# Attention and mixture-of-experts block on one core: routing arithmetic in the rank bank, plain fp32 products, and a re-laid order of slots and transfers

## The chip, the core and the metric

One core of one Trainium2 chip runs the whole program. The metric is the device time of one execution in microseconds (us), the median of several runs. The hardware profiler recorded one more execution of the kernel before.

## What is computed

128 sequences of 128 rows with 256 features: a layer norm, differential cross-attention onto a context (16 heads, 32 half-heads of 8 dimensions), a residual, a second layer norm, and a mixture of 16 experts with two chosen per row, plus a shared expert.

```
x = x + xattn(ctx, layernorm(x))   # att = softmax(q1 k1) - lam * softmax(q2 k2), 16 heads
scores = sigmoid(h @ gate_w.T)                           # h = layernorm(x), 16 experts
topk_w, topk_idx = top_k(scores, 2)
topk_w = topk_w / (topk_w.sum(-1) + 1e-20) * 2.5
routed = sum over the two experts of w * (silu(h @ w_gate) * (h @ w_up)) @ w_down
shared = silu(h @ ws_gate) * (h @ ws_up) @ ws_down
x = x + routed + shared
```

## The kernel before

The program has two stages. The first takes the 128 sequences two at a time: 64 **steps**, software-pipelined over every engine. The second runs 144 tiles of expert rows, twice.

In a step each engine walks 16 **slots** k = 0 to 15 (`step`, one function for each engine). On TensorE a slot is four score matmuls of sequence pair `it` and four matmuls of pair `b` = it+1 whose maxima VectorE takes (`both`, L477 and L470), then `attend` every second slot (L510), then `side`: the work of other pairs that is hung on this slot. ScalarE takes the exponential of a slot's scores (L783) and then its own side work; VectorE the maxima (L916) and side work. Each engine runs its list strictly in order. The letters: `a` = it+3 (projection of queries and keys), `xs` = it+4 (first norm), `n2`, `k2` = it+2, `d` = it-1 (second norm, transposes), `r` = it-2 (routing, shared expert, scatter).

Four PSUM banks carry side work: M0 and M1 (`ms_ps`), OT and TO (`o_ps`). `clear` makes TensorE wait until the previous user of a bank has been read. TO holds in turn the transposed outputs, the transposed maxima and the **rank bank** contents: the matmuls of L617 and L618 give every row its rank among the rows of its expert, and the totals.

Routing of pair r: ScalarE's exp (`ez`), VectorE's `best_two` (slot 2), `choice` (slot 3, one-hot rows `hot`, and `hots`, signed by the direction in which an expert's list grows), TensorE's ranks (slot 5), `places` (slot 6) and `positions` (slot 8), then four indirect DMAs by GpSimd (`scatter`). Several small VectorE operations read and write SBUF alone: `den`, `hots`, `hotp`.

Products of the first stage are made of three single-pass fp32r matmuls of high and low parts (`product`, L538 to L540), the shared expert's gate and up and the router's logits among them; VectorE makes the low part `h_lo` for these.

Queries and keys are cut into three bf16 parts: ScalarE writes the first, GpSimd the second (L1230) and third (L1232), SyncE puts them to DRAM (`put_parts`) and loads them as stacks (`load_stacks`). The row maxima go into the stacks as two more rows (`put_max`, from `mxT`, which ScalarE copies at slots 2 and 11). Slot 8 of TensorE waits for the DMA semaphores of both:

```
if k % 4 == 0:
    wait(pe, d_stk[u][1 - k // 4 % 2], STK, b, STK)
wait(pe, v_red, NCH, b, k - 1)
...
if do_c and k % (NCH // 2) == 0:
    wait(pe, d_m[u], MR, it, MR)
```

## Time and profile before

| | us |
|---|---|
| median of 3 runs (2449.36 to 2455.13) | 2450.85 |
| the profiled execution, its own time | 2456.25 |
| its span | 2454.5 |
| TensorE busy, share of the span | 2113.0, 86% |
| VectorE busy | 1754.8, 71% |
| GpSimd busy | 1494.5, 61% |
| ScalarE busy | 1406.2, 57% |

TensorE's matmuls overlap each other, so that its busy time is the time in which at least one was under way. The granted clock is the share of full TensorE speed (2.4 GHz) that the chip gave: 1.0 or, for stretches, 0.5. The idle time in a row is what the engine stood still right before these instructions, and the names behind the arrow say what ended it. A step ends where the next one's first exponential starts.

### The profile page before, as it was taken

How to read it: one execution, taken by the hardware profiler on the slowest of the kernel's cores; microseconds unless marked ns; L12 is line 12 of the kernel's file. 1: busy time of each engine (PE TensorE's matmuls, PEld its weight loads, DVE VectorE, ACT ScalarE, POOL GpSimd, SP SyncE). 2: the span in 40 equal slices, each digit the busy share in tenths (PEclk: the TensorE clock that was granted, in tenths of full speed). 3: DMA queues.
4: the chain of work that ended last, by engine and by line, in shares of the span. 5: the costliest groups of instructions: out<-in, count | busy, mean ns of one | idle time of the engine just before them, and what ended most of it. 6: DMA issues, size and time to landing. Idle time of an engine off the chain costs nothing.

```text
span 2454.5 us, 78894 instructions
## 1 busy us (share of the span) xinstructions
PE 2113.0 (86%) x20781; PEld 1497.9 (61%) x20782; DVE 1754.8 (71%) x4835; ACT 1406.2 (57%) x3432; POOL 1494.5 (61%) x2313
## 2 busy tenths in 40 slices
PE   4788898888898888898888898998884899979997
PEld 3456666555565555666566565666652677658886
DVE  3567888888888877888878888888753566544443
ACT  2556666666666656666666666666652444435443
POOL 5355666666666666666666666666633355445555
PEclk7788989999999989989989989999976899989999
DMA  5566556556555555555555555555614888867784
GB/s 137 164 193 179 167 159 168 158 156 171 168 165 158 171 165 147 162 155 168 165 158 161 157 167 164 162 157 157 180 57 149 252 271 279 250 211 228 225 237 148
DMA packets 583282, 432.52 MB, mean 176 GB/s; under 512 B 434070, under 2 KB 507930, under 8 KB 582688
## 3 DMA queue, kind: packets, MB, share of 16 engines
q1 hardware_dynamic: 547872, 342.28, 50.0%
q0 software_dynamic: 30720, 84.99, 9.5%
q10 hardware_dynamic: 4608, 4.26, 0.5%
q8 instruction: 39, 0.64, 0.1%
q14 instruction: 43, 0.35, 0.0%
HBM read 235.18 MB, written 200.47 MB: 177 GB/s over the span
## 4 chain that ended last, share of the span: by engine, by line
PE 37%; issue 18%; SPq 14%; DVE 9%; ACT 7%; POOL 6%; DMA 6%; ACTq 2%; POOLq 1%; DVEq 0%; another core or an unknown queue 0%
PE mx_ps L477 6%; PE ms_ps L538 5%; DMA stacks<-mxT 5%; PE o_ps L510 5%; PE ms_ps L539 4%; PE ms_ps L540 4%; PE mx_ps L722 3%; SPq L328 3%; SPq L375 3%; DVE mx L916 2%; PE o_ps L521 2%; SPq L449 2%; SPq L448 2%; SPq L368 2%; POOL out L1324 2%
## 5 line engine op out<-in xcount | busy, mean ns | idle before, releaser
L783 ACT ACTIVATE prob<-st_ps 128x512 f32<-128x512 f32 x1024 | 624.4, 610 | 626.1 <-PE st_ps L470 574.0
L916 DVE TENSOR_REDUCE mx<-mx_ps 128x4 f32<-128x512 f32 x1024 | 702.4, 687 | 215.2 <-PE mx_ps L477 191.5
L477 PE MATMUL mx_ps<-stacks 48*128 48x128 bf16 x4096 | 412.3, 227 | 59.3 <-DMA stacks<-mxT 43.7
L470 PE MATMUL st_ps<-stacks 50*128 50x128 bf16 x4096 | 412.1, 227 | 0.9 <-issue 0.9
L510 PE MATMUL o_ps<-prob,v_sb 128*32 128x256 f32 x4096 | 349.4, 415 | 21.7 <-ACT oT L774 21.6
L477 PEld LDWEIGHTS mx_ps<-stacks 48*128 48x128 bf16 x4096 | 240.1, 97 | 207.1 <-issue 116.8
L722 PE MATMUL mx_ps<-w_gu_sb,prob 128*128 x1152 | 306.1, 389 | 3.0 <-ACT prob L853 2.3
L1120 DVE TENSOR_TENSOR prob<-prob,mx_ps 128x128 f32<-128x128 f32 x288 | 82.9, 288 | 239.9 <-ACT prob L858 192.8
L1320 POOL DMA_INDIRECT rows_dram<-stacks x144 | 141.8, 985 | 171.4 <-DVE stacks L1114 137.3
L470 PEld LDWEIGHTS st_ps<-stacks 50*128 50x128 bf16 x4096 | 238.7, 97 | 4.2 <-issue 3.1
L722 PEld LDWEIGHTS mx_ps<-w_gu_sb,prob 128*128 128x128 f32 x1152 | 199.0, 192 | 22.0 <-issue 3.7
L1324 POOL DMA_INDIRECT out<-stacks x144 | 141.7, 984 | 111.4 <-issue 86.8
L853 ACT ACTIVATE prob<-st_ps 128x256 f32<-128x256 f32 x288 | 110.8, 385 | 168.1 <-PE st_ps L714 91.1
L1241 POOL TENSOR_TENSOR att<-o_sc 128x128 f32<-128x128 f32 x256 | 117.9, 461 | 136.6 <-DVE o_sc L936 131.9
L1271 POOL DMA_INDIRECT rows_dram<-rowt,posi x128 | 131.9, 1031 | 87.8 <-issue 69.1
L521 PE MATMUL o_ps<-ident,oT 128*128 128x128 f32 x1024 | 175.4, 296 | 1.0 <-issue 0.8
L735 PE MATMUL ms_ps<-w_dn_sb,v_sb 128*128 x576 | 172.8, 383 | 0.8 <-issue 0.5
L858 ACT ACTIVATE prob<-mx_ps 128x128 f32<-128x128 f32 x288 | 80.1, 278 | 156.2 <-PE mx_ps L722 117.7
L1269 POOL DMA_INDIRECT base_dram<-rowt,posi x128 | 134.6, 1051 | 56.6 <-ACT rowt L765 35.4
L714 PE MATMUL st_ps<-ident,stacks 128*128 128x128 f32 x576 | 116.6, 285 | 58.5 <-DMA stacks<-base_dram 39.3
L521 PEld LDWEIGHTS o_ps<-ident,oT 128*128 128x128 f32 x1024 | 112.2, 145 | 73.4 <-issue 60.5
L1248 POOL TENSOR_TENSOR x<-att,x_res 128x128 f32<-128x128 f32 x256 | 117.2, 458 | 61.3 <-POOL att L1241 58.2
...
## 6 DMA issues: line engine op xcount, KB each, us to landing
stacks<-stack_dram SPq DMA_DIRECT2D x512, 192.0 KB
stacks<-rows_dram SPq DMA_DIRECT2D x144, 260.0 KB
stack_dram<-kp SPq DMA_DIRECT2D x128, 256.0 KB, 4.5
...
stacks<-rows_dram SPq DMA_DIRECT2D x144, 132.0 KB
stacks<-base_dram SPq DMA_DIRECT2D x144, 128.0 KB
...
```

The lines of the kernel that those rows point to most:

```text
L470: return pe.matmul(st_ps[k % 2][:, i * P:(i + 1) * P], k_st[p][64 * h:64 * h + KROWS, u, j, :], q_st[p][64 * h:64 * h + KROWS, u, j, :], s ...
L477: return pe.matmul(mx_ps[k % 2][:, i * P:(i + 1) * P], q_st[p][64 * h:64 * h + ROWS, u, j, :], k_st[p][64 * h:64 * h + ROWS, u, j, :], sta ...
L510: mm = pe.matmul(OT[SLOT * g:SLOT * (g + 1), gg * SW:(gg + 1) * SW], v_sb[s.par()][:, (u * HEADS + 2 * c + i) * SLOT:(u * HEADS + 2 * c + ...
L521: mm = pe.transpose(out_ps, src, ident[:, :])
L722: mm = pe.matmul(gu_ps[t.off % 2][:, 0:2 * HID], rows_T[t.off % 4][:, h * P:(h + 1) * P], w_gu_sb[:, bass.ds(up, 1), h, :].rearrange("p e ...
L735: pe.matmul(eo_ps[t.off % 2][:, 0:D], hid_T[t.off % 4][:, :], w_dn_sb[:, bass.ds(down, 1), :].rearrange("p e n -> p (e n)"), start=True, s ...
L783: nc.scalar.activation(prob[k % 4][:, :], st_ps[k % 2][:, :], ACT.Exp, scale=float(HALF) ** -0.5).then_inc(a_exp, 1)
L916: v.tensor_reduce(mx[:, u, c * CHUNK:(c + 1) * CHUNK], mx_ps[k % 2][:, :].rearrange("p (c n) -> p c n", c=CHUNK), AX.X, ALU.max).then_inc( ...
L1269: g.indirect_dma_start(base_dram[:, :], at, rowt[p][:, u, 0:D], None).then_inc(d_scat[p], 16)
L1271: g.indirect_dma_start(rows_dram[:, :], at, rowt[p][:, u, D:RW], None).then_inc(d_scat[p], 16)
L1320: g.indirect_dma_start(rows2_dram[:, :], bass.IndirectOffsetOnAxis(ap=row.bitcast(U32)[:, C_POS:C_POS + 1], axis=0), row[:, :], None, boun ...
L1324: g.indirect_dma_start(out_rows, bass.IndirectOffsetOnAxis(ap=row.bitcast(U32)[:, C_TOK:C_TOK + 1], axis=0), row[:, 0:D], None, bounds_che ...
```

## The change

- `gate_up` and `logits` are plain fp32 matmuls of the one transposed tile `h2T`; the split weights, `h_hi`, `h_lo` and VectorE's subtraction for them are gone.
- The ranks come from the unsigned `hot`; `hots`, `den` and their steps are gone. The starting positions carry the sign from the setup on, and the position is the absolute value at the end (a multiply and maximum with two inputs in place of a cast). The sum of the two weights, its guard and its reciprocal are made in PSUM, in the columns of TO behind the ranks, at slot 7; `hotp` reads PSUM. The 1 is added to `ez` by a reduction over pairs.
- Slots: ranks 5 to 6, shared down product 7 to 8, second-norm transposes 13 to 12; on ScalarE `x_hi` and `ez` 1 to 0, the maxima's copy 2 to 1, the second norm 11 to 10, `h` 14 to 13, the first norm 15 to 13; on VectorE the statistics of x from 10 to 1.
- The bf16 cast of the second part of queries and keys goes from GpSimd to ScalarE (slots 11 and 2). GpSimd takes the terms of both norms together, counts row numbers in place, and does the q part after the first two scatters.
- SyncE puts the maxima ahead of the stack loads, and loads x ahead of the query parts.

```diff
@@ SyncE, step @@
+        if it.is_in(0, NS):
+            put_max(it, 1)
         if b.is_in(0, NS):
             wait(sp, p_st, NCH, it)
             load_stacks(b, 1, 1)
             load_stacks(b, 1, 0)
-        if it.is_in(0, NS):
-            put_max(it, 1)
...
-        if a.is_in(0, NS):
-            wait(sp, g_qs, 1, a, 1)
-            put_parts(a, 0, qp, d_qw)
         if xs.plus(1).is_in(1, NS):
             wait(sp, a_n1, 2, xs, 2)
...
+        if a.is_in(0, NS):
+            wait(sp, g_qs, 1, a, 1)
+            put_parts(a, 0, qp, d_qw)
@@ TensorE @@
     def gate_up(k):
         for h in range(DK):
-            mm = product(M1[:, k * SW:(k + 1) * SW], [w[:, h, k * HID:(k + 1) * HID] for w in (ws_hi, ws_lo)],
-                         [t[:, h, :] for t in (h_hi, h_lo)], h == 0, h == DK - 1)
+            mm = pe.matmul(M1[:, k * SW:(k + 1) * SW], ws_gu_sb[:, h, k * HID:(k + 1) * HID], h2T[:, h, :],
+                           start=(h == 0), stop=(h == DK - 1))
...
-                mm = product(M0[:, u * E:(u + 1) * E], [t[:, h, u * P:(u + 1) * P] for t in (h_hi, h_lo)],
-                             [w[:, h, :] for w in (gw_hi, gw_lo)], h == 0, h == DK - 1)
+                mm = pe.matmul(M0[:, u * E:(u + 1) * E], h2T[:, h, u * P:(u + 1) * P], gw_sb[:, h, :],
+                               start=(h == 0), stop=(h == DK - 1))
...
-        if k == 5 and do_r:
+        if k == 6 and do_r:
             clear(it, "TO", 2)
             wait(pe, v_hot, 1, r, 1)
-            flat = hots[:, :, :].rearrange("p u e -> p (u e)")
+            flat = hot[:, :, :, :].rearrange("p u k e -> p (u k e)")
...
-        if k == 7 and do_r:
+        if k == 8 and do_r:
             clear(it, "M0", 2)
             wait(pe, v_sh, 1, r, 1)
...
-        if k == 13 and do_d:
+        if k == 12 and do_d:
             clear(it, "M1", 3)
@@ ScalarE, step @@
-            if k == 1 and do_a:
+            if k == 0 and do_a:
...
-            if k == 1 and do_r:
+            if k == 0 and do_r:
...
-                nc.scalar.activation(ez[:, :], M0[:, 0:2 * E], ACT.Exp, scale=-1.0).then_inc(a_e, 1)
+                nc.scalar.activation(ez[:, :, 0], M0[:, 0:2 * E], ACT.Exp, scale=-1.0).then_inc(a_e, 1)
...
-            if k == 2 and do_c:
+            if k == 1 and do_c:
                 copy_max(it, 1)
+            if k == 2 and do_k:
+                wait(act, g_kr, 1, k2, 1)
+                nc.scalar.activation(kp[:, 1, :], k_rest[:, :], ACT.Copy).then_inc(a_kb, 1)
...
-            if k == 8 and do_r:
+            if k == 9 and do_r:
                 wait(act, p_sd, 1, r, 1)
...
-            if k == 11 and do_b:
-                copy_max(b, 0)
-            if k == 11 and do_d:
+            if k == 10 and do_d:
                 wait(act, p_hT, 1, d)
                 wait_par(act, d_scat, SCAT, d.plus(-2))
                 norm(d, x2[d.par()], mv2, nb2, rowt[d.par()][:, :, D:2 * D], g_nb2, a_n2)
+            if k == 11 and do_b:
+                copy_max(b, 0)
+            if k == 11 and do_a:
+                wait(act, v_q, 1, a, 1)
+                nc.scalar.activation(qp[:, 1, :], q_rest[:, :], ACT.Copy).then_inc(a_qb, 1)
...
-            if k == 14 and do_d:
+            if k == 13 and do_d:
...
-                nc.scalar.activation(rnd(h_hi[:, :, :]), M1[:, :], ACT.Copy).then_inc(a_h, 1)
-            if k == 15 and do_xs:
+                nc.scalar.activation(h2T[:, :, :], M1[:, :], ACT.Copy).then_inc(a_h, 1)
+            if k == 13 and do_xs:
@@ VectorE @@
-        v.tensor_scalar(ez1[:, :], ez[:, :], 1.0, None, ALU.add).then_inc(v_rt, 1)
+        v.tensor_reduce(ez1[:, :], ez[:, :, :], AX.X, ALU.add).then_inc(v_rt, 1)
...
     def places(s):
...
+        place = TO[:, 0:2 * E2]
+        both, safe, part = (TO[:, 4 * E2 + 2 * i:4 * E2 + 2 * i + 2] for i in range(3))
         wait(dve, p_pf, 1, s, 1)
+        v.tensor_reduce(both, top[:, :, 0:TOPK], AX.X, ALU.add).then_inc(v_rt, 1)
         v.tensor_tensor(base[:, 1, :], base[:, 0, :], tot[:, 0, :], ALU.add).then_inc(v_ps, 1)
+        wait(dve, v_rt, RT, s, 8)
+        v.tensor_scalar(safe, both, 1e-20, None, ALU.add).then_inc(v_rt, 1)
         wait(dve, v_ps, 3, s, 1)
-        v.tensor_tensor(pb[:, :, :], TO[:, 0:2 * E2].rearrange("p (u e) -> p u e", u=2), base[:, :, :],
-                        ALU.add).then_inc(v_ps, 1)
+        v.tensor_tensor(place.rearrange("p (u e) -> p u e", u=2), place.rearrange("p (u e) -> p u e", u=2),
+                        base[:, :, :], ALU.add).then_inc(v_ps, 1)
+        wait(dve, v_rt, RT, s, 9)
+        v.reciprocal(part, safe).then_inc(v_rt, 1)
...
     def positions(s):
...
-        v.tensor_copy(posi[s.par()][:, :], row[:, :, C_POS]).then_inc(v_pos, 1)
+        v.scalar_tensor_tensor(posi[s.par()][:, :], row[:, :, C_POS], -1.0, row[:, :, C_POS], ALU.mult,
+                               ALU.max).then_inc(v_pos, 1)
     def step(it):
...
-            if k == 1 and do_a:
+            if k == 0 and do_a:
                 low(a, M1, a_x, x_hi, x_lo, v_x)
+            if k == 1 and do_xs:
+                wait(dve, d_x, 16, xs, 16)
+                stats(xs, x_in, bs1, mv1, v_b1, v_s1, a_n1)
...
-            if k == 10 and do_xs:
-                wait(dve, d_x, 16, xs, 16)
-                stats(xs, x_in, bs1, mv1, v_b1, v_s1, a_n1)
-            if k == 11 and do_a:
+            if k == 10 and do_a:
                 rest(a, M1, a_q, qp, q_rest, g_qs, v_q)
-            if k == 14 and do_d:
-                low(d, M1, a_h, h_hi, h_lo, v_hl)
@@ GpSimd @@
-        g.tensor_copy(part[:, 1, :], tmp[:, :]).then_inc(g_b, 1)
-        wait(gp, g_b, 1, s, 1)
+    def split(s, tmp, part, a_second, g_done):
+
+        wait(gp, a_second, 1, s, 1)
         g.tensor_tensor(part[:, 2, :], tmp[:, :], part[:, 1, :], ALU.subtract).then_inc(g_done, 1)
```

How this moves the instructions, at three places. SyncE around the start of step 3, before (`stacks<-stack_dram` is `load_stacks(b, 1, ...)`, `stacks<-mxT` is `put_max(it, 1)`, `kp` the key parts):

```order
L375 DMA stacks<-stack_dram 48x1x2048 [waits p_st]
L375 DMA stacks<-stack_dram 48x1x2048 x3
L383 DMA stacks<-mxT 2x16x128 [waits a_mT]
L383 DMA stacks<-mxT 2x16x128
L368 DMA stack_dram<-kp 128x8x128 [waits d_stk10,d_stk01,d_stk11,d_stk00,g_ks]
```

and now:

```order
L375 DMA stacks<-mxT 2x16x128 [waits a_mT]
L375 DMA stacks<-mxT 2x16x128
L367 DMA stacks<-stack_dram 48x1x2048 [waits p_st]
L367 DMA stacks<-stack_dram 48x1x2048 x3
L360 DMA stack_dram<-kp 128x8x128 [waits d_stk10,d_stk01,d_stk11,d_stk00,g_ks]
```

The two transfers of the maxima stand ahead of the four stack loads, and so wait for `a_mT` alone.

VectorE from the end of `best_two` through `choice` to the next pair of maxima, before:

```order
L967 MAX_INDEX topi<-top,score 128x8
L968 SCALAR_TENSOR_TENSOR den<-top 128x2
L916 TENSOR_REDUCE mx<-mx_ps 128x4 [waits p_mx]
L974 CAST rowt<-topi 128x2x2 [waits v_rt]
L976 TENSOR_TENSOR hot<-iota_e,rowt 128x64 [waits v_rt]
L980 RECIPROCAL rden<-den 128x2 [waits v_rt]
L982 TENSOR_TENSOR hots<-hot,sign_b 128x64 [waits v_one]
L985 SCALAR_TENSOR_TENSOR rowt<-top,rden 128x2x2 [waits v_rt]
L916 TENSOR_REDUCE mx<-mx_ps 128x4 [waits p_mx]
```

and now:

```order
L964 MAX_INDEX topi<-top,score 128x8
L913 TENSOR_REDUCE mx<-mx_ps 128x4 [waits p_mx]
L970 CAST rowt<-topi 128x2x2 [waits v_rt]
L972 TENSOR_TENSOR hot<-iota_e,rowt 128x64 [waits v_rt]
L913 TENSOR_REDUCE mx<-mx_ps 128x4 [waits p_mx]
```

Of six operations between the two sets of maxima two are left; the weights' division has gone behind the ranks.

GpSimd in step 3 from the residual of pair `it` to its next part, before (`qp<-q_rest` the second and third query part):

```order
L1248 TENSOR_TENSOR x_1<-att,x_res 128x128 [waits g_base,a_n2,d_res1,g_att]
L1269 DMA base_dram<-rowt,posi 133120x256 [waits a_n2,v_rt,g_tok,g_base,v_pos]
L1190 TENSOR_SCALAR ve<-mv 128x2 [waits v_s1]
L1192 TENSOR_TENSOR mv<-ve,neghalf 128x2 [waits g_ve1]
L1198 TENSOR_SCALAR nb<-mv 128x1 [waits g_r1]
L1198 TENSOR_SCALAR nb<-mv 128x1
L1271 DMA rows_dram<-rowt,posi 133120x264 [waits a_n2,v_rt,g_tok,g_base,v_pos]
L1230 CAST qp<-q_rest 128x512 [waits d_qw,v_q]
L1232 TENSOR_TENSOR qp<-q_rest,qp 128x512 [waits g_qb]
L1269 DMA base_dram<-rowt,posi 133120x256 [waits a_n2,v_rt,g_tok,g_base,v_pos]
L1241 TENSOR_TENSOR att<-o_sc 128x128 [waits g_x2,v_cb]
```

and now:

```order
L1247 TENSOR_TENSOR x_1<-att,x_res 128x128 [waits g_base,a_n2,d_res1,g_att]
L1264 DMA rows_dram<-rowt,posi 133120x264 [waits v_pf,v_pos]
L1262 DMA base_dram<-rowt,posi 133120x256 [waits g_base]
L1231 TENSOR_TENSOR qp<-q_rest,qp 128x512 [waits a_qb]
L1264 DMA rows_dram<-rowt,posi 133120x264
L1240 TENSOR_TENSOR att<-o_sc 128x128 [waits g_x2,v_cb]
```

The query part waits for ScalarE's cast (`a_qb`) and stands behind two indirect DMAs as before, but the four operations of the first norm and the cast are no longer ahead of it.

## Rows read from the trace of the kernel before

**Rows 1.** Stretches: busy us (instructions), clock, DMA share, GB/s; head, 56 steps, three steps.
```profile
core 0: us, PE busy (x) PEld busy (x) DVE busy (x) ACT busy (x) POOL busy (x), PEclk, DMA share, GB/s
66.20:217.10 150.90, 122.23 (x1345) 81.97 (x1344) 94.53 (x240) 86.52 (x190) 73.57 (x127) 0.84 0.62 182
217.10:1768.00 1550.90, 1373.29 (x15904) 936.37 (x15904) 1296.36 (x3300) 1015.74 (x2239) 1050.39 (x1735) 0.94 0.57 162
793.40:820.80 27.40, 23.20 (x284) 15.82 (x284) 23.62 (x60) 18.24 (x42) 18.85 (x32) 1.00 0.59 165
907.00:934.70 27.70, 25.88 (x284) 18.14 (x284) 21.11 (x59) 18.03 (x41) 14.92 (x28) 0.88 0.56 155
967.60:992.70 25.10, 23.10 (x284) 15.82 (x284) 21.02 (x59) 18.02 (x41) 16.24 (x29) 1.00 0.63 174
```

**Rows 2.** Groups by form, 217.1 to 1768: TensorE, idle time before and its releasers.
```profile
L477 PE MATMUL mx_ps<-stacks 48*128 48x128 bf16 x3584 | 356.8, 225 | 30.0 <-DMA stacks<-mxT 22.7 <-DVE mx L916 4.5 <-ACT prob L783 0.9
...
L623 PE MATMUL ms_ps<-ws_dn_sb,sh_h 128*128 128x256 f32 x224 | 67.7, 429 | 31.8 <-DVE sh_h L954 31.1 <-ACT v_sb L806 0.4
...
L532 PE MATMUL ms_ps<-ident,xn 128*128 128x128 f32 x224 | 36.9, 287 | 50.3 <-ACT xn L765 45.9 <-DVE h_lo L903 4.4
...
L617 PE MATMUL o_ps<-hots,upper 128*128 128x64 bf16 x56 | 11.4, 203 | 34.7 <-DVE o_sc L936 34.5
```

**Rows 3.** Timeline of one step from 793.4: SyncE, start, length.
```profile
802.41 1.41 SPq L383 DMA_DIRECT2D stacks<-mxT  x2
```

**Rows 4.** Chain of waits, same step.
```profile
803.17 5.38 DMA stacks<-mxT
```

**Rows 5.** Timeline, TensorE: logits, gate and up of the step, expert stage; start, length.
```profile
794.01 0.26 PE L538 MATMUL ms_ps<-gw_hi,h_hi 128*128 128x16 f32 x1
...
795.42 0.23 PE L477 MATMUL mx_ps<-stacks 48*128 48x128 bf16 x1
...
801.42 0.28 PE L538 MATMUL ms_ps<-h_hi,ws_hi 128*128 128x256 f32 x1
...
802.22 0.23 PE L477 MATMUL mx_ps<-stacks 48*128 48x128 bf16 x1
...
2053.73 1.03 PE L722 MATMUL mx_ps<-w_gu_sb,prob 128*128 x4
2054.59 0.27 PE L730 MATMUL o_ps<-ident,prob 128*128 128x128 f32 x1
```

**Rows 6.** Groups by form, 217.1 to 1768: VectorE and GpSimd.
```profile
L968 DVE SCALAR_TENSOR_TENSOR den<-top 128x2 f32<-128x2 f32 x56 | 50.0, 892 | 0.0
...
L1000 DVE TENSOR_TENSOR hotp<-hot,pb 128x64 f32<-128x64 bf16 x56 | 43.2, 772 | 0.0
...
L982 DVE TENSOR_TENSOR hots<-hot,sign_b 128x64 bf16<-128x64 bf16 x56 | 41.9, 748 | 0.0
...
L903 DVE TENSOR_TENSOR h_lo<-ms_ps,h_hi 128x512 fp32r<-128x512 f32 x56 | 38.7, 691 | 35.1 <-ACT h_hi L838 35.1
...
L1230 POOL CAST kp<-k_rest 128x512 bf16<-128x512 f32 x56 | 34.3, 612 | 17.6 <-POOL k_rest L1224 17.4
...
L996 DVE TENSOR_TENSOR pb<-o_ps,base 128x64 f32<-128x64 f32 x56 | 12.5, 224 | 1.9
```

**Rows 7.** Timeline from 912: VectorE, hotp at its shortest.
```profile
921.97 0.22 DVE L1000 TENSOR_TENSOR hotp<-hot,pb 128x64 f32<-128x64 bf16 x1
```

**Rows 8.** Timeline, 815.7 to 821: ScalarE at the end of a step.
```profile
815.80 0.60 ACT L783 ACTIVATE prob<-st_ps 128x512 f32<-128x512 f32 x1
...
820.76 0.66 ACT L783 ACTIVATE prob<-st_ps 128x512 f32<-128x512 f32 x1
```

**Rows 9.** Timeline from 1299: ScalarE slot 2, GpSimd; from 926: GpSimd.
```profile
1303.25 0.63 ACT L783 ACTIVATE prob<-st_ps 128x512 f32<-128x512 f32 x1
...
1304.79 1.18 POOL L1224 TENSOR_TENSOR k_rest<-k_all,kp 128x512 f32<-128x512 f32 x1
...
936.53 1.09 POOL L1271 DMA_INDIRECT rows_dram<-rowt,posi  x1 [3.42 <-issue]
```

More of the change, by code:

```diff
@@ L184, in program @@
         hot = sb("hot", [P, 2, TOPK, E], BF16)
-        hots = sb("hots", [P, 2, E2], BF16)
-        den = sb("den", [P, 2])
-        rden = sb("rden", [P, 2])
-        number = sb("number", [P, 2])
         no_row = sb("no_row", [P, RW])
@@ L591, in side @@
                     clear(it, "M0", 0)
-                    wait(pe, v_hl, 1, r, 1)
+                    wait(pe, a_h, 1, r, 1)
                     logits().then_inc(p_lg, 1)
@@ L605, in side @@
                         clear(it, "M1", 1)
-                        wait(pe, v_hl, 1, r, 1)
                     mm = gate_up(k // 2 - 1)
@@ L967, in best_two @@
                     v.max_index(topi[:, u, :], top[:, u, :], score[:, u, :]).then_inc(v_rt, 1)
-                v.scalar_tensor_tensor(den[:, :], top[:, :, 0], 1e-20, top[:, :, 1], ALU.add, ALU.add).then_inc(v_rt, 1)
             def choice(s):
                 row = rowt[s.par()]
+                wait(dve, v_rt, RT, s, 6)
+                v.tensor_copy(row[:, :, C_E:C_E + TOPK], topi[:, :, 0:TOPK]).then_inc(v_rt, 1)
                 wait(dve, v_rt, RT, s, 7)
-                v.tensor_copy(row[:, :, C_E:C_E + TOPK], topi[:, :, 0:TOPK]).then_inc(v_rt, 1)
@@ L1034, in step @@
                         stats(d, x2[d.par()], bs2, mv2, v_b2, v_s2, a_n2)
+                    if k == 7 and do_r:
+                        places(r)
                     if k == 8 and do_r:
```

151 lines of the change are left out of this document (69 added, 82 removed).

## The prediction

> **What bounds the kernel now.** I read the stretches first, then what TensorE waited for, then one step in time. The first stage's 56 steady steps take 1550.9 us, 27.69 us each; TensorE is busy for 1373.3 us of it, so it stands idle for 177.6 us, 3.17 us a step [rows 1]. A step at full clock has 23.20 us of TensorE work and lasts 27.40 us; one at a clock of 0.88 has 25.88 us and lasts 27.70 us [rows 1]. So the length is the same whether TensorE is slowed or waits: other engines' chains set the pace, and TensorE's slack is eaten by either. One step at full clock came out at 25.10 us with the same work [rows 1], which shows that nothing forces 27.4 us. Over the 56 steps the clock costs 1373.3 - 56 x 23.20 = 74 us of busy time, 1.3 us a step.
>
> The idle time is named: 50.3 us before the first-norm transposes, which wait for ScalarE's norm in slot 15; 34.7 us before the rank matmuls, for VectorE's `combine` behind the routing; 31.8 us before the shared down product, for `sh_h`; 30.0 us before the maxima, mostly for the transfer of the row maxima in slot 8 [rows 2]. That is 146.8 us; some 31 us lie elsewhere in small pieces. In the step from 793.4 SyncE issues the maxima at 802.41, behind four stack loads [rows 3], and the chain shows 5.38 us from there to the landing [rows 4], just when TensorE could go on.
>
> **The change part by part.**
>
> TensorE's own work. The logits took 12 products from 794.01 to 795.42, 1.41 us; gate and up took 6 from 801.42 to 802.22, and again 6, 1.60 us together [rows 5]. Plain fp32 appears as two records a product: two products of 256 columns take 2053.73 to 2054.59, 0.86 us [rows 5]. Gate and up have four: 1.72 us, 0.12 more. No plain product with 16 columns is in the trace. Its 8 records cost at least what a logits record costs now (1.41/12, 0.94 us) and at most 0.215 each (1.72 us); I take 0.94, because a record there is paced by its 128-column weights, as now. Net: -0.35 us a step, bounds -0.35 and +0.43. Work 22.85 us.
>
> VectorE. `den` 892, `hotp` 772 and `hots` 748 ns on the mean are far above `pb` at 224 ns, which handles as many elements from PSUM [rows 6]; at its best `hotp` takes 0.22 us [rows 7]. Something holds up operations that touch SBUF alone, while GpSimd is at work. With `den` replaced by two small operations in PSUM at 224, `hots` and `h_lo` (691 [rows 6]) gone and `hotp` at 224, VectorE saves 0.89 - 0.45 + 0.75 + 0.69 + 0.55 = 2.4 us a step. Against this, the position becomes an operation with two SBUF inputs, which may be held like `den`: 0 to 0.75 us; I take 0, as slot 8 stands behind the ranks and nobody on TensorE waits for it. The statistics of x (4 operations, the same ones) move from slot 10 to slot 1. So the routing's one-hot rows come some 1.6 us earlier by their own, and the wait for `combine` is nearly gone, all the more as the ranks are asked for one slot later; `sh_h` likewise has one slot more. Terms: 34.7 and 31.8 us, freed.
> The Trainium skill (VectorE: DVE Perf Modes, "The TRN2 errata") gives operations that read PSUM about 120 fixed cycles against 58 for SBUF, 65 ns more for each. By an estimate from that page the six operations in PSUM would cost 0.4 us a step, 22 us in all, were VectorE the bound. The trace does not bear it out: 0.22 us from SBUF at best against 224 ns with PSUM.
>
> SyncE. `put_max(it, 1)` no longer waits for the four loads; two such transfers take 1.41 us to issue [rows 3], so four loads some 2.8 us by an estimate, and its own can go out by so much sooner; the 5.38 us of landing then end before TensorE asks. Freed: 30.0 us less the 7 us that are not the transfer's. What is late next: the first stack load of slot 8, now behind the maxima where it was ahead of them, and so has 1.4 us less slack. The x load goes out ahead of the query parts and reaches VectorE's slot 1 in time only if ScalarE's norm is done by the end of slot 13.
>
> ScalarE. It runs without a pause from 815.80 to 820.76, 4.96 us, in slots 12 to 15 [rows 8]. The new list for these slots holds the same operations (`h` and the first norm come sooner), so it stays 4.96 us; but the transposes no longer wait for the norm as the last item. I free the 50.3 us (0.90 us a step) and charge 0.7 us a step because ScalarE's list is longer than TensorE's there (estimate: three of 16 slots of 22.85 us, 4.3 us). Two casts come to it, in slots 2 and 11, at about 0.6 us each; slot 2 is covered by ScalarE's idle time behind TensorE's products. Without that cover each costs TensorE 0.6 us.
>
> GpSimd loses two casts of 612 ns and more [rows 6] and does the terms of both norms together; its list gets at least 1.2 us shorter ahead of the key part, and the query part no longer stands behind the norm's operations. It has no bearing on the sum by itself; it feeds SyncE.
>
> Sum for a step: 22.85 work + 0.7 ScalarE's end + 0.55 (the small waits, 31 us / 56) + 0.7 for slow-clock windows and new waits between slots 8 and 12 = 24.8 us. The last term is chosen: half of today's 1.3 us, since most, not all, of the idle goes. 56 x (27.69 - 24.8) = 162 us. The five steps before (150.9 us, 28.7 idle [rows 1]) suffer from the same transfer, besides the expert weights' loads: a third of that, 10 us. The expert stage is not touched, nor is the setup beyond 1 us. From the profiled execution's 2456.25 us: 2456 - 172 = 2284. The median stands 5.4 us under that execution, so 2279, rounded to **2280 us**.
>
> **The rivals.**
>
> *ScalarE and the loads take over (28%).* ScalarE's 18.24 us of a step [rows 1] become some 19.4, and slots 9 to 12 now hold the shared output's copy, the second norm, a cast that waits for VectorE's `q_rest` in slot 10, and two copies of the keys; VectorE's slots 0 to 8 got the x statistics. And TensorE, sooner at slot 8, can meet the stack load. For it: ScalarE is already saturated in slots 12 to 15. Against: the 25.10 us step. A step of 26.4 us gives 56 x 1.29 = 72 us, with 5 of the head: 2374.
> The Trainium skill (SBUF — State Buffer, "Who interferes with whom") says that a VectorE operation with two SBUF inputs still contends with a GpSimd operation that reads SBUF. That would keep `hot` and the new position operation slow, and belongs to this case; the long `den` and `hotp` agree with it.
>
> *All chains clear (11%).* No slow windows, ScalarE's end hidden: 23.6 us, 56 x 4.09 + 10 = 239 less: 2212. The clock decides; the step from 793.4 kept full clock with 4.2 us of idle, so it is possible.
>
> *Slower: ScalarE is held in slot 2 (9%).* The key cast there waits for GpSimd's `k_rest`. Before, ScalarE's slot-2 exponential started at 1303.25, and `k_rest` ran from 1304.79 to 1305.97 [rows 9]: at such a place ScalarE would stand for 2.1 us with all later exponentials queued behind it, and TensorE and VectorE behind those. GpSimd also pauses up to 3.42 us before an indirect DMA [rows 9]. If GpSimd's list does not come forward by those 2.1 us, the gain is 0.9 us (first norm) against 2.1: 28.9 us a step, 56 x 1.2 = 67 us more, 2518. It decides once `k_rest` ends more than some 2 us behind ScalarE's slot 2. Against: at least 1.2 us less of GpSimd's work stands ahead of it [rows 6].
>
> *No difference (4%).* The waits are only exchanged and transfers still set 27.6 us: 2445.
>
> **How the numbers follow.** The forecast has 48%, and 2280 is its time. The range takes the clear case and the take-over nearly to its end: 2212 to 2374, widened a little below and above for the logits' bound (0.78 us x 56 = 44 us) within them: 2205 to 2390. Some 0.2% (5 us) is what a measurement can tell here. Faster by more: forecast, take-over and clear case, 0.87; within: 0.04, the case without difference, though its own value is 6 us off; slower: 0.09.
>
> **What would show it.** TensorE's idle time before the ranks, the shared down product and the first-norm transposes near zero; before the maxima, a releaser other than `mxT`; the routing operations in PSUM at about 0.2 us; granted clock above 0.96 in the steps; ScalarE's idle time smaller than 9 us a step. I am wrong if ScalarE's cast in slot 2 shows idle time ahead of it with GpSimd as releaser, if the stack loads become the maxima's releaser, or if logits take above 1.4 us.

## The result, and the profile after

| | kernel before | changed kernel |
|---|---|---|
| median, us | 2452.99 (4 runs, 2449.36 to 2469.29) | 2612.01 (4 runs, 2607.77 to 2618.66) |
| ratio, 95% interval | | 1.0637 (1.0584 to 1.069) |
| profiled span | 2454.5 | 2611.1 |

The forecast was 2280 us with a range of 2205 to 2390. The kernel is 6.4% slower: it lies outside of the range, and on the other side of the kernel before.

The stretches of the changed kernel, with the columns of [rows 1]: the head, the same 56 steps, one step, and that step's two parts.

```profile
core 0: us, PE busy (x) PEld busy (x) DVE busy (x) ACT busy (x) POOL busy (x), PEclk, DMA share, GB/s
66.60:204.10 137.50, 113.93 (x1321) 75.43 (x1322) 91.30 (x239) 92.87 (x199) 68.41 (x116) 0.92 0.69 202
204.10:1903.40 1699.30, 1501.81 (x15458) 996.30 (x15458) 1124.51 (x3245) 1078.57 (x2351) 954.88 (x1566) 0.85 0.53 148
662.30:693.00 30.70, 27.13 (x277) 17.97 (x277) 20.16 (x59) 19.27 (x42) 16.77 (x29) 0.83 0.51 146
669.10:689.60 20.50, 17.56 (x212) 11.22 (x211) 13.33 (x40) 12.46 (x27) 11.18 (x21) 1.00 0.47 134
689.60:699.90 10.30, 9.67 (x65) 6.85 (x66) 6.80 (x22) 6.81 (x16) 5.87 (x9) 0.50 0.62 170
```

The 56 steps take 1699.3 us, 30.34 each, where they took 27.69 [rows 1]: 148.4 us more. Head and last three steps are 13.4 and 14.0 us shorter. The expert stage, which the diff does not touch, is 35.2 us longer (640.0 for 604.8 us), nearly all in its second pass; with 0.4 us at the start that makes the 156.6 us between the spans. TensorE's idle time is 197.5 us, 19.9 more than the 177.6 of before. What grew most is its busy time, 1501.8 us for 1373.3 (128.5 us of the 148.4), though it has less work: the granted clock is 0.85 for 0.94. From step 6 on nearly every step is the same: 20.5 us at 2.4 GHz, then 10.2 us at 1.2 GHz, together 30.7 us. In the kernel before, the stretches at 1.2 GHz came and went and were shorter (184 us in the 56 steps, here 519).

Where TensorE waits now, groups by form of the 56 steps, to be read beside [rows 2]:

```profile
L469 PE MATMUL mx_ps<-stacks 48*128 48x128 bf16 x3584 | 383.6, 233 | 18.7 <-ACT prob L774 4.5 <-DVE mx L913 3.8 <-DMA stacks<-stack_dram 2.4
L502 PE MATMUL o_ps<-prob,v_sb 128*32 128x256 f32 x3584 | 330.9, 446 | 111.5 <-ACT oT L765 111.4
...
L513 PE MATMUL o_ps<-ident,oT 128*128 128x128 f32 x896 | 169.5, 319 | 64.1 <-DVE rowt L998 60.5 <-issue 3.5
...
L764 ACT ACTIVATE oT<-o_ps 128x256 f32<-128x256 f32 x224 | 86.4, 386 | 111.9 <-remote 82.2 <-PE o_ps L502 25.5
...
L614 PE MATMUL ms_ps<-ws_dn_sb,sh_h 128*128 128x256 f32 x224 | 63.0, 404 | 0.1
...
L524 PE MATMUL ms_ps<-ident,xn 128*128 128x128 f32 x224 | 60.0, 419 | 0.0
...
L608 PE MATMUL o_ps<-hot,upper 128*128 128x64 bf16 x56 | 11.4, 203 | 0.0
```

All four waits that I set out to free are gone or nearly so: 0.0 us before the first-norm transposes (L524, was 50.3), 0.0 before the ranks (L608, 34.7), 0.1 before the shared down product (L614, 31.8), 18.7 before the maxima (30.0) with `mxT` no longer named. In their place stand two that the prediction does not have: 111.4 us before the attend matmuls (L502) for ScalarE's `oT`, which itself waits 82.2 us for "remote", a releaser that the profile can't name; and 60.5 us before the transposes of the outputs (L513) for VectorE's `rowt` of L998, the weights that close the places.

The first one in a single step, on the timelines of ScalarE, VectorE, GpSimd and TensorE (start, length):

```profile
687.09 0.62 ACT L774 ACTIVATE prob<-st_ps 128x512 f32<-128x512 f32 x1
689.33 0.38 ACT L764 ACTIVATE oT<-o_ps 128x256 f32<-128x256 f32 x1 [1.62 <-remote]
```

```profile
687.85 0.42 DVE L933 TENSOR_TENSOR o_sc<-o_ps,rl 128x256 f32<-128x256 f32 x1
689.33 0.69 DVE L913 TENSOR_REDUCE mx<-mx_ps 128x4 f32<-128x512 f32 x1 [1.06 <-PE mx_ps L469]
```

```profile
686.39 1.10 POOL L1264 DMA_INDIRECT rows_dram<-rowt,posi  x1 [0.60 <-issue]
687.80 0.96 POOL L1262 DMA_INDIRECT base_dram<-rowt,posi  x1 [0.30 <-issue]
688.79 1.16 POOL L1231 TENSOR_TENSOR qp<-q_rest,qp 128x512 bf16<-128x512 f32 x1
```

```profile
686.86 0.64 PE L502 MATMUL o_ps<-prob,v_sb 128*32 128x256 f32 x8
...
687.84 0.22 PE L469 MATMUL mx_ps<-stacks 48*128 48x128 bf16 x1
...
690.13 0.66 PE L502 MATMUL o_ps<-prob,v_sb 128*32 128x256 f32 x4 [1.90 <-ACT oT L765]
```

TensorE issued the attend matmuls of slot 13 at 686.86 and the maxima of slots 14 and 15 by 688.1. ScalarE, free from 687.71, goes on at 689.33; VectorE, free from 688.27, at 689.33 too. Both wait for semaphores that TensorE raises, and both stand idle 1.0 to 1.6 us beyond the modelled ends of its matmuls, until the same moment. This happens in every step from 5 to 58, but for one. As the profile models these ends, it can't tell whether the results themselves or only their semaphores came late. At just that time GpSimd has issued two indirect DMAs with nothing between them, at 686.39 and 687.80; in the kernel before, the norm's four operations stood between. TensorE then idles for 1.90 us, and at 689.6 its clock falls.

VectorE's groups went as forecast, to be read beside [rows 6]:

```profile
L989 DVE TENSOR_TENSOR o_ps<-o_ps,base 128x64 f32<-128x64 f32 x56 | 13.0, 233 | 0.0
...
L995 DVE TENSOR_TENSOR hotp<-hot,o_ps 128x64 f32<-128x64 bf16 x56 | 12.0, 215 | 0.0
...
L1008 DVE SCALAR_TENSOR_TENSOR posi<-rowt 128x2 uint32<-128x2 f32 x56 | 9.7, 173 | 4.5
L992 DVE RECIPROCAL o_ps<-o_ps 128x2 f32<-128x2 f32 x56 | 9.5, 169 | 0.0
```

`hotp` takes 215 ns for 772, the position's two-input operation 173 ns (I had bounds of 0 to 0.75 us above its old time, and took 0). Beside what these operations were slow can be read in the trace of before, instruction by instruction: `den` took 142 ns on the mean in the 9 steps in which no GpSimd operation ran beside it, and 938 in the 40 in which only `k_rest` did; `hots` 192 (23 steps) and 1072 (35, beside `att` and the third key part).

### The profile page after: what moved, and what is told of

Read it like the earlier page. It is cut to its first block, busy times and chain, and to the rows that moved or that the text cites. A ratio compares the mean times of both kernels' runs of the same rounds, so it can differ in the third digit from the quotient of the medians.

```text
span 2611.1 us, 76352 instructions
## 1 busy us (share of the span) xinstructions
PE 2231.3 (85%) x20269; PEld 1539.1 (59%) x20270; DVE 1569.5 (60%) x4770; ACT 1467.6 (56%) x3558; POOL 1387.5 (53%) x2121
## 4 chain that ended last, share of the span: by engine, by line
PE 59%; ACT 10%; issue 9%; SPq 8%; DVE 6%; another core or an unknown queue 3%; DMA 2%; ACTq 2%; POOL 0%; DVEq 0%; POOLq 0%
PE mx_ps L469 9%; PE o_ps L502 9%; PE mx_ps L713 6%; PE ms_ps L530 6%; PE o_ps L513 5%; PE ms_ps L551 5%; PE ms_ps L559 3%; PE ms_ps L531 3%; PE ms_ps L532 3%; ACT prob L774 3%; PE ms_ps L726 3%; PE ms_ps L524 2%; DVE mx L913 2%; ACT oT L765 2%
## 5 line engine op out<-in xcount | busy, mean ns | idle before, releaser
L774 ACT ACTIVATE prob<-st_ps 128x512 f32<-128x512 f32 x1024 | 602.7, 605 | 501.5 <-PE st_ps L462 481.2
L469 PE MATMUL mx_ps<-stacks 48*128 48x128 bf16 x4096 | 438.9, 233 | 49.5 <-DMA stacks<-stack_dram 20.0
L502 PE MATMUL o_ps<-prob,v_sb 128*32 128x256 f32 x4096 | 374.3, 442 | 117.0 <-ACT oT L765 116.4
L462 PE MATMUL st_ps<-stacks 50*128 50x128 bf16 x4096 | 437.7, 233 | 0.3 <-ACT prob L774 0.3
L469 PEld LDWEIGHTS mx_ps<-stacks 48*128 48x128 bf16 x4096 | 250.3, 100 | 277.0 <-issue 183.3
L513 PE MATMUL o_ps<-ident,oT 128*128 128x128 f32 x1024 | 192.8, 318 | 69.6 <-DVE rowt L998 60.5
L513 PEld LDWEIGHTS o_ps<-ident,oT 128*128 128x128 f32 x1024 | 124.1, 157 | 173.1 <-issue 81.8
L502 PEld LDWEIGHTS o_ps<-prob,v_sb 128*32 128x32 f32 x4096 | 85.2, 114 | 184.6 <-ACT oT L765 138.9
L1231 POOL TENSOR_TENSOR kp<-k_rest,kp 128x512 bf16<-128x512 f32 x64 | 74.1, 1158 | 204.6 <-ACT kp L790 204.6
L1220 POOL TENSOR_TENSOR c_lo<-c_in,c_hi 128x512 fp32r<-128x512 f32 x64 | 81.0, 1266 | 171.1 <-ACT c_hi L807 171.1
```

The source lines that it names most:

```text
L462: return pe.matmul(st_ps[k % 2][:, i * P:(i + 1) * P], k_st[p][64 * h:64 * h + KROWS, u, j, :], q_st[p][64 * h:64 * h + KROWS, u, j, :], s ...
L469: return pe.matmul(mx_ps[k % 2][:, i * P:(i + 1) * P], q_st[p][64 * h:64 * h + ROWS, u, j, :], k_st[p][64 * h:64 * h + ROWS, u, j, :], sta ...
L502: mm = pe.matmul(OT[SLOT * g:SLOT * (g + 1), gg * SW:(gg + 1) * SW], v_sb[s.par()][:, (u * HEADS + 2 * c + i) * SLOT:(u * HEADS + 2 * c + ...
L513: mm = pe.transpose(out_ps, src, ident[:, :])
L774: nc.scalar.activation(prob[k % 4][:, :], st_ps[k % 2][:, :], ACT.Exp, scale=float(HALF) ** -0.5).then_inc(a_exp, 1)
```

## The experiments

All were compared with the kernel before on the same chip. The chips differ: on most the kernel before takes 2449 to 2456 us, on one it took 2405. A wait is **late** when ScalarE or VectorE, idle, saw TensorE's result over 0.3 us after the end that the profile models, and a step is **held** when such a wait was over 0.9 us late. Counts are of the 64 steps; a table of all traces follows behind the experiments on adjacency.

### Four edits, on the chip where the kernel before takes 2405 us

The scatters are the indirect DMAs of GpSimd. The first two apart (`a_apart`), the places ahead of the statistics (`a_places`), both (`a_both`), and the reverse edit in the kernel before (`b_adjacent`):

```diff
@@ GpSimd, a_apart @@
-                if do_c:
-                    residual(it, 0)
                 if do_r:
                     ...
                     scatter(r, 0, 1)
+                if do_c:
+                    residual(it, 0)
+                if do_r:
                     wait(gp, g_base, 1, r, 1)
                     scatter(r, 0, 0)
@@ VectorE, a_places @@
+                    if k == 7 and do_r:
+                        places(r)
                     if k == 7 and do_d:
                         ...
                         stats(d, x2[d.par()], bs2, mv2, v_b2, v_s2, a_n2)
-                    if k == 7 and do_r:
-                        places(r)
@@ GpSimd, b_adjacent (the kernel before) @@
-                if do_r:
-                    scatter(r, 0, 0)
                 if do_xs:
                     deviation(xs, mv1, v_s1, g_ve1, g_r1)
                     shift(xs, mv1, nb1, g_r1, g_nb1)
                 if do_r:
+                    scatter(r, 0, 0)
                     scatter(r, 0, 1)
```

> The changed kernel, with the residual's first half between the first two scatters instead of ahead of both; nothing else. In the changed kernel GpSimd issues two indirect DMAs back to back (686.39 and 687.80), and TensorE's results of 687.5 to 688.2 reach ScalarE and VectorE only at 689.25 and 689.33, 1.5 us late. Theory 'back-to-back scatters hold TensorE': the delay before ScalarE's oT in slot 13 falls from 1.6 us to 0.7 us or less, the step no longer locks at 30.72 us, the granted clock rises above 0.9 and the time falls to 2500 or less. Rival 'the delay belongs to TensorE's own list of slots 12 to 14': the delay stays at 1.5 us and the time within 15 us of 2612.

> The changed kernel, with the routing's places ahead of the statistics of x in VectorE's slot 7. In the changed kernel TensorE waits 1.25 us at slot 8 for the bank TO until VectorE's weights are written behind those statistics (1.1 us). Theory: that wait goes, TensorE's first gap is under 0.4 us; if the clock only needs less idle time, the step leaves 30.72 us and the time falls by 30 us or more. Rival 'the low clock hangs on the gap in slot 14 alone': the gap of slot 8 goes, the slow stretches stay (clock 0.83), and the step is shorter by at most 1.1 us, or not at all if its length is tied to the clock's steps: 2550 to 2612.

> Both edits of the two runs before in one kernel. If both waits are what TensorE lost, the step has 22.3 us of work and under 1.5 us of idle: 25 us or less, 2330 or less in all, near my forecast of 2280. If the clock still falls once in a step, 27 to 28 us a step, 2440 to 2480.

> The kernel before, with its first two scatters back to back (the terms of the first norm ahead of both). Theory 'back-to-back scatters hold TensorE': a delay of some 1.5 us of TensorE's results appears in each step where one of up to 0.8 us stood, slower by 10 to 100 us. Rival: no more than 5 us of change.

Measured: a_apart 2351.2, ratio 0.9795 (0.9741 to 0.9849); a_places 2327.0, 0.9692 (0.9642 to 0.9742); a_both 2308.7, 0.962 (0.9571 to 0.9669); b_adjacent 2386.3, 0.9943 (0.9917 to 0.9969). This settled nothing: every edit seemed to heal the kernel, and the scatters back to back left the kernel before the same or 0.6% faster, where the theory had it slower. In a_places they are back to back as in the changed kernel, and no wait in the steps is late:

```profile
L764 ACT ACTIVATE oT<-o_ps 128x256 f32<-128x256 f32 x224 | 86.5, 386 | 13.3 <-PE o_ps L502 7.7
```

The same holds for all four traces of this chip. Either the chip does not show the effect, or I had the wrong one. What was missing is the changed kernel itself beside its edits, on one chip.

### The same kernels where the kernel before takes 2450 us

> The changed kernel as it is, again, beside the kernel before, since in the last four runs the kernel before took 2405 us where it took 2453 in the first comparison. If the loss is in the kernel whatever the chip, the ratio is again 1.05 to 1.07, with TensorE's results of slot 14 seen 1.0 us late or more in nearly every step and 30.7 us a step. If the loss hangs on what this chip does around GpSimd's indirect DMAs, and the edits of the last runs had little to do with it, the ratio is 0.96 to 0.99, steps of 26 to 27 us, and no late results at slot 14.

> The kernel before as it is, with a profile on the chip of this call. Ratio 1.00. On the first chip its steps took 27.7 us with 58 late releases, those by TensorE in slots 3 and 13 up to 0.8 us late; where it runs at 2405 us, the steps should take 27.0 us and the late releases of slots 3 and 13 should be gone, if these are what tells the chips apart.

c_after: 2607.9, 1.0601 (1.0555 to 1.0648). c_before: 2449.9, 0.9983 (0.995 to 1.0017). The loss repeats, with 116 waits late and 53 steps held. The kernel before has late waits too, 32, but only 3 steps are held. What I expected of c_before where it takes 2405 us stays untested.

> The changed kernel again, now in one call with its two edits, on whatever chip it is. Where the kernel before takes 2450: 2600 to 2620, steps of 30.7 us, late results at slot 14. Where it takes 2405 (no late results in the four runs there): if the late results are what makes the loss, 2370 to 2400, the clock not locked at 0.833; if the order of the scatters or the places' wait made it, still above 2500.

> The changed kernel with the first two scatters apart, as a_apart. Where the kernel before takes 2450 and the late results exist: if the two adjacent scatters are what holds TensorE, the lateness in slot 14 falls under 0.8 us and the time to 2400 or less; if it is the chip's and the place's alone, within 15 us of the changed kernel. Where the kernel before takes 2405: 2351 again.

> The changed kernel with the places ahead of the statistics, as a_places. Where the kernel before takes 2450: the gap of slot 8 goes (1.2 us a step) but results are still late at slot 14 by 1.0 us; the step either stays at 30.7 us (length tied to the clock's steps) or falls to 26 to 27.5 us: 2360 to 2450. Where the kernel before takes 2405: 2327 again.

> The changed kernel with both edits, as a_both. Where the kernel before takes 2450: 2340 to 2380 if both waits are what was lost. Where it takes 2405: 2309 again.

Measured, all on one chip: d_after 2617.5, 1.07 (1.0642 to 1.0759); **d_apart 2423.9, 0.9904 (0.9873 to 0.9934)**; d_places 2620.9, 1.0702 (1.0644 to 1.0761); d_both 2416.7, 0.9873 (0.9795 to 0.9951). One residual between two scatters (0.9 us of work; from the end of the first to the start of the second 1.7 us for 0.3) takes 194 us off. Still, d_apart and d_both lie above the 2400 and the 2340 to 2380 that I expected of them. In d_apart no step is held before step 60. ScalarE's `oT` of slot 1 is still late in 51 steps, by 0.3 to 0.7 us in all but one, beside a scatter that stands alone; `oT` waits 39.1 us in all and for nothing unnamed, and the clock is back at 0.94, with short stretches at 1.2 GHz (178 us in all):

```profile
208.90:1732.20 1523.30, 1367.37 (x15458) 911.10 (x15458) 1125.54 (x3243) 1074.72 (x2351) 953.56 (x1565) 0.94 0.59 165
```

```profile
L469 PE MATMUL mx_ps<-stacks 48*128 48x128 bf16 x3584 | 361.9, 223 | 78.9 <-ACT prob L774 59.4 <-DMA stacks<-stack_dram 11.5 <-DVE mx L913 3.4
L502 PE MATMUL o_ps<-prob,v_sb 128*32 128x256 f32 x3584 | 295.2, 401 | 26.1 <-ACT oT L765 18.7 <-issue 7.4
...
L513 PE MATMUL o_ps<-ident,oT 128*128 128x128 f32 x896 | 150.8, 292 | 48.1 <-DVE rowt L998 45.8 <-issue 2.3
...
L764 ACT ACTIVATE oT<-o_ps 128x256 f32<-128x256 f32 x224 | 86.4, 386 | 39.1 <-PE o_ps L502 34.8 <-issue 0.3
```

In d_places TensorE's wait for the bank fell from 62.6 us (d_after) to 10.8, and the time did not move at all. Its steps are still 30.7 us:

```profile
205.20:1909.10 1703.90, 1517.90 (x15458) 1004.04 (x15458) 1124.00 (x3245) 1078.16 (x2351) 952.34 (x1565) 0.84 0.53 148
```

```profile
L469 PE MATMUL mx_ps<-stacks 48*128 48x128 bf16 x3584 | 395.9, 238 | 59.2 <-ACT prob L774 53.3 <-DVE mx L913 2.7 <-issue 1.0
L502 PE MATMUL o_ps<-prob,v_sb 128*32 128x256 f32 x3584 | 320.9, 434 | 112.2 <-ACT oT L765 112.0
...
L513 PE MATMUL o_ps<-ident,oT 128*128 128x128 f32 x896 | 147.8, 288 | 11.5 <-DVE rowt L998 10.8 <-issue 0.6
```

The freed 52 us turn up before the maxima (53.3 us for ScalarE's `prob`). With the slow stretch in every step, taking away this wait elsewhere in it bought nothing. What the changed kernel itself would take on the chip with 2405 us was not measured.

### Does adjacency do it, or its place?

e_before_adjacent is b_adjacent again. e_pair_later moves the pairs of the changed kernel, and e_sync_undone is d_apart with SyncE's order as before:

```diff
@@ GpSimd, e_pair_later @@
                     wait(gp, g_tok, 1, r, -1)
-                    scatter(r, 0, 1)
                     wait(gp, g_base, 1, r, 1)
-                    scatter(r, 0, 0)
                 if do_a:
                     split(a, q_rest, qp, a_qb, g_qs)
                 if do_r:
-                    scatter(r, 1, 1)
+                    scatter(r, 0, 1)
+                    scatter(r, 0, 0)
                 if do_c:
                     residual(it, 1)
                 if do_r:
+                    scatter(r, 1, 1)
                     scatter(r, 1, 0)
@@ SyncE, e_sync_undone @@
-                if it.is_in(0, NS):
-                    put_max(it, 1)
                 if b.is_in(0, NS):
                     wait(sp, p_st, NCH, it)
                     load_stacks(b, 1, 1)
                     load_stacks(b, 1, 0)
+                if it.is_in(0, NS):
+                    put_max(it, 1)
```

> The kernel before with its first two scatters back to back, as b_adjacent, which ran where no results were late. Here, if the kernel before takes 2450: theory 'two adjacent scatters hold TensorE for 1.5 us': late results of over 0.9 us in most steps and a time of 2465 or more. Rival 'adjacency is not enough, the place in TensorE's slot matters (TensorE's results must fall due behind the scatter's start)': no change beyond 15 us.

> The changed kernel with both pairs of scatters adjacent, the first pair behind the third query part (1.2 us later) and the second behind the residual. If adjacency holds TensorE wherever it stands: late results of 1.0 us or more, only at another slot (15 or 0), and 2550 or more where the kernel before takes 2450. If the place decides: late results under 0.5 us and 2400 to 2450.

e_before_adjacent: 2484.4, 1.0133 (1.0039 to 1.0227), 33 us above the kernel before beside it. The time came as the theory has it, the waits did not: 5 steps are held, not most. e_pair_later: 2434.9, 0.9931 (0.9884 to 0.9978). Here the waits came, 58 steps held and by up to 1.8 us, and the time did not: I expected 2550 or more.

Both fit when all results of TensorE are counted, waited for or not. The second column of the table pairs its semaphore updates in the 64 steps, some 3750 to 4020 of them, with the modelled ends; where the trace lacks an update, the oldest result is left out.

| kernel | results over 0.9 us late (steps with one) | steps held |
|---|---|---|
| changed kernel, three traces | 224 to 229 (56 to 57) | 53 to 54 |
| d_places | 231 (59) | 55 |
| g_pair_back (below) | 234 (57) | 54 |
| e_before_adjacent | 236 (61) | 5 |
| e_pair_later | 430 (61) | 58 |
| kernel before, two traces | 32 (15 to 16) | 2 to 3 |
| scatters apart: d_apart, d_both, e_sync_undone | 8 to 10 (3 to 4) | 0 to 2 |
| scatters apart (below): e_norm_later | 43 (27) | 1 |
| f_load_first, f_load_first_norm13, g_places_back | 8 to 19 (3 to 12) | 0 to 1 |
| the four traces where the kernel before takes 2405 | 0 to 2 (0 to 2) | 0 |

Except on that chip, adjacent scatters hold TensorE's results wherever they stand; the price hangs on who needs them then. So adjacency alone does not make the loss: the changed kernel puts the pair where ScalarE's `oT`, for which TensorE waits, falls due. In e_pair_later, 1.2 us later, ScalarE has work at that moment, and TensorE's gap in slot 15 is 1.0 to 1.2 us, not 1.9; VectorE pays the 1.7 us out of its own slack. GpSimd and VectorE in one step of e_pair_later:

```profile
340.16 1.10 POOL L1264 DMA_INDIRECT rows_dram<-rowt,posi  x1 [0.17 <-issue]
341.57 0.96 POOL L1262 DMA_INDIRECT base_dram<-rowt,posi  x1 [0.30 <-issue]
```

```profile
343.06 1.29 DVE L913 TENSOR_REDUCE mx<-mx_ps 128x4 f32<-128x512 f32 x2 [1.70 <-remote]
```

> The changed kernel with the scatters apart (as d_apart, 2424 where the kernel before takes 2450), and with the row maxima again behind the four stack loads on SyncE. My step 'the 5.38 us of landing end before TensorE asks' says that this order is worth up to 0.5 us a step (30.0 us in all): 2435 to 2460, TensorE waiting for the transfer of the maxima before slot 8. If the transfer hides anyway: within 10 us of 2424.

e_sync_undone: 2459.9, 1.0031 (0.9993 to 1.0069), 36 us above d_apart (the kernel before took 2451.7 beside the one and 2450.5 beside the other). The transfer of the maxima is back as a releaser:

```profile
L469 PE MATMUL mx_ps<-stacks 48*128 48x128 bf16 x3584 | 363.9, 224 | 115.8 <-ACT prob L774 63.3 <-DMA stacks<-mxT 44.8 <-DVE mx L913 7.0
```

### Why the rest gives 27 us a step and not 24.8

In d_both TensorE waits 81.7 us for ScalarE's exponentials at the end of the step. e_norm_later is d_both with the first norm one slot later; f_load_first is that with two of the stack loads ahead of the maxima; f_load_first_norm13 has the loads' order alone on top of d_both:

```diff
@@ ScalarE, e_norm_later @@
-                    if k == 13 and do_xs:
+                    if k == 14 and do_xs:
@@ SyncE, f_load_first @@
-                if it.is_in(0, NS):
-                    put_max(it, 1)
                 if b.is_in(0, NS):
                     wait(sp, p_st, NCH, it)
                     load_stacks(b, 1, 1)
+                if it.is_in(0, NS):
+                    put_max(it, 1)
+                if b.is_in(0, NS):
                     load_stacks(b, 1, 0)
```

> The changed kernel with both edits (as d_both, 2417 where the kernel before takes 2450), and with the first norm in ScalarE's slot 14, behind its exponential, instead of 13. In d_both TensorE still waits 1.0 us at the end of each step for the exponential of slot 14, which stands behind the norm's 1.1 us on ScalarE. If that wait is real loss: it falls under 0.3 us and the time by 20 to 55 us, to 2360 to 2395. If ScalarE's whole list sets the end of the step: the wait moves to the next exponential or to the transposes, within 10 us of 2417.

> e_norm_later (scatters apart, places first, first norm in slot 14) with SyncE issuing the first two stack loads ahead of the maxima, and the other two behind: they wait only for scores that are done when the step begins, while the maxima wait for ScalarE's copy in slot 1. In e_norm_later TensorE waits 86.3 us for those loads at slot 8. Theory 'what is late next is the first stack load': that wait goes, the step falls from 27.3 to 25.5 us or less and the time to 2330 or less where the kernel before takes 2450. Rival 'the transfers share one bandwidth, and order changes nothing': the wait moves to the maxima or to slot 12, within 15 us of 2423.

> The same order of SyncE with the first norm left in slot 13 (as d_both, 2417 where the kernel before takes 2450, where the loads cost TensorE 24.9 us and ScalarE's exponential 83.0). If ScalarE's end sets these steps, 2390 to 2420; if both had to go together, this one gains less than f_load_first by 20 us or more.

e_norm_later: 2423.4, 0.9876 (0.9814 to 0.9939), nothing gained. The wait changed its name, from the exponential to the stack loads:

```profile
L469 PE MATMUL mx_ps<-stacks 48*128 48x128 bf16 x3584 | 356.3, 220 | 112.7 <-DMA stacks<-stack_dram 86.3 <-ACT prob L774 16.9 <-DVE mx L913 3.6
```

**f_load_first: 2278.5, 0.9289 (0.9215 to 0.9362)**, the fastest version of this study. f_load_first_norm13: 2342.2, 0.9545 (0.9468 to 0.9622). The two waits stood side by side: against d_both, taking either alone gives 0 and 75 us, both together 138. The two with the loads' order ran on another chip than d_both, with the kernel before at 2449.4 and 2450.5 us. The stretch, TensorE's groups and SyncE's timeline of f_load_first:

```profile
211.60:1578.80 1367.20, 1287.70 (x15458) 852.27 (x15456) 1116.68 (x3244) 1071.31 (x2351) 953.12 (x1566) 1.00 0.66 184
```

```profile
L470 PE MATMUL mx_ps<-stacks 48*128 48x128 bf16 x3584 | 351.5, 218 | 36.8 <-DMA stacks<-mxT 24.5 <-DVE mx L914 6.7 <-DMA stacks<-stack_dram 1.0
L503 PE MATMUL o_ps<-prob,v_sb 128*32 128x256 f32 x3584 | 286.3, 391 | 21.5 <-issue 12.2 <-ACT oT L766 8.7
...
L514 PE MATMUL o_ps<-ident,oT 128*128 128x128 f32 x896 | 145.7, 285 | 3.7 <-DVE rowt L999 2.1 <-issue 0.6
```

```profile
1022.87 1.52 SPq L367 DMA_DIRECT2D stacks<-stack_dram  x2
1024.62 1.40 SPq L375 DMA_DIRECT2D stacks<-mxT  x2
1026.06 1.57 SPq L367 DMA_DIRECT2D stacks<-stack_dram  x2
```

24.41 us a step, idle for 79.5 us of 1367.2, and the clock at 2.4 GHz throughout. SyncE used to sit idle here: in the changed kernel from 695.3 to 698.24, until ScalarE's copy of the maxima was there. The first two loads need nothing of that step and fit into the pause.

Last, f_load_first with one of the changed kernel's two waits put back:

> f_load_first (2278 where the kernel before takes 2450) with the first two scatters back to back again, as in the changed kernel. If adjacency costs only where it leaves TensorE idle, this now tells: with a shorter step the held results of 1.0 to 1.5 us return, the clock falls again in most steps, and the time is 2350 or more; the worst case is a lock at 0.833 as in the changed kernel, 2600. Rival: the other edits gave the slack that hides it, within 15 us of 2278.

> f_load_first with the places behind the statistics again, as in the changed kernel. In d_apart against d_both that cost 7 us, though TensorE's wait for the bank TO stood there (52.2 against 5.6 us). If it was hidden by the low clock, it is worth its full size now: TensorE waits 0.9 to 1.2 us before slot 8's transposes, 2330 or more. If it is still hidden, within 15 us of 2278.

g_pair_back: 2474.9, 1.0101 (1.0001 to 1.02): 196 us lost by the order of one residual and one scatter, the clock at 0.88. g_places_back: 2307.3, 0.9405 (0.9328 to 0.9481), 29 us more than f_load_first, with a wait of 51.4 us before L514; I expected 2330 or more if that wait had its full price. In the changed kernel it cost nothing (d_places).

```profile
210.40:1799.10 1588.70, 1456.17 (x15458) 967.21 (x15456) 1119.47 (x3245) 1071.57 (x2352) 950.69 (x1565) 0.88 0.57 158
```

```profile
L514 PE MATMUL o_ps<-ident,oT 128*128 128x128 f32 x896 | 146.8, 286 | 55.0 <-DVE rowt L999 51.4 <-issue 3.6
```

## Why the prediction was wrong

By its sum the change takes 172 us off; 159 us were added. So it is not a size that was off but the mechanism. **The step that failed** is the one on GpSimd: "It has no bearing on the sum by itself; it feeds SyncE." I counted what left GpSimd's list (two casts) and not what then stood next to what. The norm's operations left the gap between the first two indirect DMAs, and that held TensorE's results by some 1.5 us in 54 of 64 steps; with the gap back (d_apart) the same kernel takes 194 us less. The order in front of the prediction shows the two scatters adjacent, and the trace of before shows the effect in small: one scatter was issued at 433.58, TensorE's maxima of 434.27 should have been done at 434.49, and VectorE, idle, took them at 435.31. I had put such lateness down to small pieces.

```profile
433.58 1.10 POOL L1269 DMA_INDIRECT base_dram<-rowt,posi  x1 [0.78 <-ACT rowt L765]
...
434.27 0.22 PE L477 MATMUL mx_ps<-stacks 48*128 48x128 bf16 x1
...
435.31 0.69 DVE L916 TENSOR_REDUCE mx<-mx_ps 128x4 f32<-128x512 f32 x1 [1.01 <-PE mx_ps L477]
```

**The clock.** I charged 0.7 us a step "for slow-clock windows and new waits"; the clock alone cost more. TensorE is busy 26.82 us a step where full clock would give 22.99 (f_load_first), 3.8 us. The fall comes with the gap of 1.90 us at the end of the step, and this gap comes back once a step in the same place. With gaps of 1.0 us there (d_apart) the clock is 0.94, with 0.3 us (f_load_first) 1.00. These versions differ in more than that gap, so what part of the fall is due to it alone is not shown.

**The bank TO.** I wrote that the ranks' wait would be nearly gone because they are "asked for one slot later", and it is. But ranks, `places` and the next user of TO are a chain, and I moved two of its links towards the third: the transposes of slot 8. The part of the sum that is missing is 60.5 us of idle time; g_places_back prices it at 29 us where the clock does not hide it.

**What held.** The four waits went to zero or, before the maxima, to 18.7 us. TensorE's work: 22.85 us forecast, 22.99 in f_load_first. In f_load_first the logits took 0.89 us to the next matmul (1018.58 to 1019.47, eight records) for my 0.94, but the plain gate and up took 0.95 us a half (672.38 to 673.33), 1.90 and not 1.72. SyncE's order: 23 us forecast, 36 measured. ScalarE's end: 0.7 us a step charged, 1.1 (d_apart, 59.4 us) to 1.5 (d_both, 81.7 us) measured. The cast in ScalarE's slot 2, the mechanism of my slower rival, waited for GpSimd for 1.2 us in all 56 steps; so that slower came out in sign, and for another reason than the rival's: luck. The rival "ScalarE and the loads take over" (28%, 2374) is what d_apart, d_both and e_norm_later show, at 2417 to 2424. Of my signs for the forecast the granted clock (0.85, not above 0.96) and ScalarE's idle time (11.1 us a step, not under 9) failed; of my three signs of being wrong none came: they looked at other places than the one that failed.

**The two rules.** The Trainium skill (VectorE: DVE Perf Modes, "The TRN2 errata") would add 65 ns to each operation that reads PSUM. The trace does not agree: the reciprocal of two columns took 156 ns in SBUF (L980 of the kernel before) and 169 ns in PSUM (L992), 13 ns more. Its other rule (SBUF — State Buffer, "Who interferes with whom") was to keep the new position operation slow; it took 173 ns. In 60 of the 64 steps GpSimd's power operation on two columns ran over it (in the step shown from 679.33 to 680.71, the position at 679.54), and it took 172 ns then and 161 in the one step with nothing beside it, so at these small sizes the rule does not show. With `den` and `hots`, beside GpSimd operations of 0.5 to 1.2 us, the trace agrees with it.

That f_load_first takes 2278 us, the forecast's number, proves no step of it: it has four edits that are not in the change, and that it lands on that number is luck.

**Open.** What in an indirect DMA holds TensorE's results, and why one chip did not show it, was not tried. The 35 us of the expert stage come from its second pass, which from its first tile to the end of the span took 256.4 us before and 290.9 after, though its instructions are the same. Its length goes with the late waits in it: 3 in the trace of before (4 us in all) and 61 in the changed kernel's (47 us). In the other traces of the changed kernel and its versions it is 28 to 33 late waits and 269 to 272 us, or 60 to 66 and 285 to 292 us; where the kernel before takes 2405 us it is none and 252 to 253 us. No run changed this stage, so the link is argued, and why two traces of one kernel differ in it (290.9 and, in d_after, 271.4 us) is open.
